# Two accumulator banks for projections and one for head turns, loads in four pieces, and GpSimd in the output rounding of a fused cross-attention kernel

## The reference: what is computed

```
ln_out = LN(x);  q, k, v, qx = fp8_linear(ln_out, each with its own input scale)   # rounded to e4m3
q, k, qx, kx = LN over each head of 128;  kx, vx from ctx @ w_kv_x (fp32)
core = softmax(q k^T / sqrt(128)) v;   xout = softmax(qx kx^T / sqrt(128)) vx      # 8 groups, 2 heads each
cat  = concat(core, xout);  catq = e4m3(bf16(clip(cat / smooth, -448, 448)))
x += tanh(g0) * (catq @ wproj^T) * scales
x += tanh(g1) * bitlinear(silu(gate) * up)
```

## Time and profile before

| | before |
|---|---|
| median of the runs | 1891.02 us |
| profiled execution, its own time | 1892.87 us |
| its span from first to last instruction | 1891.1 us |
| first and last score matmul start | 109.3 us, 1535.7 us |
| TensorE busy | 1640.8 us, 87% |
| VectorE busy | 1567.0 us, 83% |
| ScalarE busy | 1353.8 us, 72% |
| GpSimd busy | 1092.9 us, 58% |
| mean granted TensorE clock | 0.967 |

### The profile page before, as it was taken

One profiled execution on the slowest core, in us unless ns is written; L12 is line 12 of the kernel. 1 busy time (PEld: TensorE's weight loads), 2 busy tenths in 40 slices (PEclk: granted clock), 3 DMA queues, 4 the chain that ended last, 5 costly groups with the idle time before them and its releaser, 6 DMA issues.

```text
span 1891.1 us, 35124 instructions
## 1 busy us (share of the span) xinstructions
PE 1640.8 (87%) x11147; PEld 1012.6 (54%) x11164; DVE 1567.0 (83%) x3445; ACT 1353.8 (72%) x3351; POOL 1092.9 (58%) x1427
## 2 busy tenths in 40 slices
PE   1478888788989998889999888999999879999995
PEld 0355555555656665556666555666666524444442
DVE  7668888998888889978888998999988866777774
ACT  6468888777878987887898778999888852222222
POOL 3677887776777767776776567777676630000000
PEclk9879999999999999999999999999999999999997
DMA  2367888778999998889999997999999985422200
GB/s 97 106 151 152 188 186 188 170 175 179 217 217 203 208 216 187 184 184 211 208 225 193 209 199 177 223 234 230 220 212 187 194 176 207 111 79 73 73 18 17
DMA packets 667677, 325.48 MB, mean 172 GB/s; under 512 B 551904, under 2 KB 595040, under 8 KB 666720
## 3 DMA queue, kind: packets, MB, share of 16 engines
q1 hardware_dynamic: 667488, 323.17, 75.9%
HBM read 140.61 MB, written 48.23 MB: 100 GB/s over the span
## 4 chain that ended last, share of the span: by engine, by line
PE 34%; DVE 32%; POOL 13%; issue 8%; ACT 8%; DMA 3%; SPq 0%; POOLq 0%; ACTq 0%; DVEq 0%
DVE nmx L963 6%; DVE pp L973 6%; PE psum L736 6%; PE psum L711 6%; PE psum L682 5%; PE psum L694 5%; PE psum L649 4%; PE psum L656 3%; PE psum L753 3%; DMA pt<-pp 2%; POOL qk L1555 2%; POOL ars L1533 2%; DVE cc L985 2%; PE psum L669 2%; DVE xh L946 2%
## 5 line engine op out<-in xcount | busy, mean ns | idle before, releaser
L682 PE MATMUL psum<-qk 128*128 128x512 f16 x1536 | 426.5, 388 | 17.1 <-DVE pp L973 12.5
L649 PE MATMUL psum<-wbt,xqt 128*128 128x256 f16 (+1 forms) x4096 | 412.0, 251 | 23.8 <-POOL wbt L1502 13.4
L694 PE MATMUL psum<-pt,vv 128*128 128x512 f16 x1536 | 405.5, 388 | 31.0 <-ACT cy L1327 21.7
L1308 ACT ACTIVATE psum<-psum,nmx 128x512 f32<-128x512 f32 x512 | 343.1, 670 | 104.6 <-DVE nmx L963 102.8
L649 PEld LDWEIGHTS psum<-wbt,xqt 128*128 128x128 f16 x4096 | 334.1, 100 | 136.0 <-issue 21.8
L963 DVE TENSOR_REDUCE nmx<-psum 128x1 f32<-128x512 f32 x512 | 345.6, 675 | 58.7 <-PE psum L682 57.7
L973 DVE SCALAR_TENSOR_TENSOR pp<-psum,prs,pp 128x512 f16<-128x512 f32 x512 | 379.0, 740 | 7.1 <-ACT pp L1319 6.9
L1319 ACT ACTIVATE pp<-psum,prs 128x512 f16<-128x512 f32 x512 | 355.2, 694 | 14.8 <-DMA pt<-pp 14.4
L694 PEld LDWEIGHTS psum<-pt,vv 128*128 128x128 f16 x1536 | 151.1, 100 | 226.8 <-issue 57.0
L1555 POOL TENSOR_TENSOR qk<-y,qk 128x512 f16<-128x512 f32 x192 | 233.8, 1218 | 16.0
L656 PE MATMUL psum<-wbt,ctxh 128*128 128x256 f16 x1536 | 193.3, 277 | 8.7 <-POOL ctxh L1481 8.7
(11 more groups left out here) (175 smaller groups left out, 2696.1 us busy)
## 6 DMA issues: line engine op xcount, KB each, us to landing
wbt<-ws SPq DMA_DIRECT2D x192, 256.0 KB, 3.7
ws<-wbt SPq DMA_DIRECT2D x64, 256.0 KB, 4.0
catd<-cy SPq DMA_DIRECT2D x64, 256.0 KB, 3.4
raw<-in_wgu SPq DMA_DIRECT2D x64, 256.0 KB, 3.6
raw<-in_w SPq DMA_DIRECT2D x32, 384.0 KB, 3.8
wbt<-catd SPq DMA_DIRECT2D x6, 2048.0 KB, 9.9
pt<-pp SPq DMA_TRANSPOSE x512, 3.7
raw<-in_wp SPq DMA_DIRECT2D x32, 256.0 KB, 3.6
```

Source lines behind the costliest of these rows:

```text
L649: ins = e.matmul(bank[:, o0:o0 + c1 - c0], xv[:, v, kt * 512 + tt * 128:kt * 512 + (tt + 1) * 128], wb[i][:, h, kt, c0:c1], start=kt == 0 ...
L682: ins = e.matmul(SB(n), qk[i][:, jq, u, ss], qk[i][:, jk, w, :], start=k == 0, stop=k == 2)
L694: ins = e.matmul(OB, v[:, t, u, att, :], src[:, w, t, :], start=t == 0 and k == 0, stop=t == 3 and k == 2)
L1308: e.activation(SB(n), SB(n), ACT.Exp, bias=nmx[:, k], accum_out=psm[:, k]).then_inc(s["exp"], 1)
```

## The change

1. Banks: after slot -4 banks 5 and 6 hold A and B tiles alone, in turn, and bank 7 holds everything else (T, X, W, C, S, F). Before slot -4 the first list is 5, 6, 0, 1, 2, 3.
2. The loads of x and of the context are four DMAs of 256 KB each, in slots 1 to 4 and 62 to 65; who reads them waits for all four. The statistics of x move from slots 4, 6, 8, 10 to 6, 8, 9, 10.
3. The turns X move from slots 20, 36, 52, 60 to 20, 26, 36, 52; the context's factor `cxf` from slot 86 to 85.
4. ScalarE writes all four quarters of `ctxh` high in slot 102 (before: two in 102, two in 103). GpSimd makes two quarters of the low part in slot 102, VectorE the other two in slot 103.
5. `group_factors` moves from n modulo 16 = 7 to 4, and S and F readers (SCALE_AT, FLAG_AT) by one or two slots.
6. All output steps lie one slot later: clip at n modulo 8 = 2, field 3, step 4, add 5, sub 6 and 0, store 3. From pair 18 (group 9) on GpSimd makes the step, so 46 of the 64; new semaphores o_f and o_s link field, step and add.

```diff
-FACTORS_AT = 7
+FACTORS_AT = 4
...
-OUT_AT = {"clip": 17, "field": 18, "step": 19, "add": 20, "sub": (21, 23), "store": 26}
+OUT_AT = {"clip": 18, "field": 19, "step": 20, "add": 21, "sub": (22, 24), "store": 27}
+POOL_STEP = 9 * 2
 JOBS_FROM, TERN_FROM = 92, 309
-SCALE_AT = {"sum": 303, "whole": 308, "fac": 310}
-FLAG_AT = {"sum": 306, "whole": 324, "fac": 326}
+SCALE_AT = {"sum": 303, "whole": 307, "fac": 308}
+FLAG_AT = {"sum": 306, "whole": 324, "fac": 325}
 X_AT = {
-    "load": (1,),
-    "stats": (4, 6, 8, 10),
+    "load": (1, 2, 3, 4),
+    "stats": (6, 8, 9, 10),
     "rstd": (10,),
     "norm": (13, 14, 15, 16),
-    "turn": (20, 36, 52, 60),
-    "ctx": (62,),
+    "turn": (20, 26, 36, 52),
+    "ctx": (62, 63, 64, 65),
     "quant": tuple(range(62, 102)),
     "bound": (70, 72, 74, 76),
     "cxp": (82,),
     "cxs": (83,),
     "cxw": (84,),
-    "cxf": (86,),
+    "cxf": (85,),
     "mid": (90, 92, 94, 96),
-    "parts": (102, 102, 103, 103),
+    "parts": (102, 102, 102, 102),
...
-    turn = [5, 6, 7, 0, 1, 2, 3]
+    long, short = [5, 6, 0, 1, 2, 3], [7]
     for n, use in order:
         if n >= RAMP:
-            turn = [k for k in turn if k >= 5]
+            long = [k for k in long if k >= 5]
+        turn = long if use[0] in "AB" else short
         k = turn.pop(0)
         turn.append(k)
         bank[use] = k
...
-            def load_x(b):
+            def load_x(b, t):
                 q.wait_ge("cx_lo", 4 * b)
-                e.dma_start(xt[:], x[b * S:(b + 1) * S, :].rearrange("(t p) d -> p t d", p=128)).then_inc(s["x_ld"], 16)
-
-            def load_ctx(b):
+                e.dma_start(xt[:, t, :], x[b * S + t * 128:b * S + (t + 1) * 128, :]).then_inc(s["x_ld"], 16)
+
+            def load_ctx(b, kt):
                 q.wait_ge("x_tr", 4 * b + 4)
-                e.dma_start(xt[:], ctx[b]).then_inc(s["ctx_ld"], 16)
+                e.dma_start(xt[:, kt, :], ctx[b][:, kt, :]).then_inc(s["ctx_ld"], 16)
...
+            def ctx_lo(b, kt):
+                q.wait_ge("cx_hi", 4 * b + kt + 1)
+                e.tensor_tensor(ctxh[:, 1, kt, :], xt[:, kt, :], ctxh[:, 0, kt, :], ALU.subtract).then_inc(s["cx_lo"], 1)
...
-            def out_step(pair, step):
-
-                y, tmp = cy[pair % 3][:], cc[:]
+            def out_field(pair):
+
                 q.wait_ge("o_c", pair + 1)
-                q.wait_ge("o_w", 3 * pair + step)
-                if step == 0:
-                    q.wait_ge("o_q", 2 * pair)
-                    ins = e.tensor_scalar(tmp.bitcast(U16), y.bitcast(U16), 0x7F80, None, ALU.bitwise_and)
-                elif step == 1:
-                    ins = e.tensor_scalar(tmp, tmp, 24.0, 0.375, ALU.mult, ALU.max)
-                else:
-                    ins = e.tensor_tensor(y, y, tmp, ALU.add)
-                ins.then_inc(s["o_w"], 1)
+                q.wait_ge("o_q", 2 * pair)
+                e.tensor_scalar(cc[:].bitcast(U16), cy[pair % 3][:].bitcast(U16), 0x7F80, None, ALU.bitwise_and).then_inc(s["o_f"], 1)
+
+            def out_step(pair):
+                q.wait_ge("o_f", pair + 1)
+                e.tensor_scalar(cc[:], cc[:], 24.0, 0.375, ALU.mult, ALU.max).then_inc(s["o_s"], 1)
+
+            def out_add(pair):
+                q.wait_ge("o_s", pair + 1)
+                e.tensor_tensor(cy[pair % 3][:], cy[pair % 3][:], cc[:], ALU.add).then_inc(s["o_w"], 1)
...
-                for k, step in enumerate(("field", "step", "add")):
-                    for pair in pairs_at(n, OUT_AT[step]):
-                        out_step(pair, k)
+                for pair in pairs_at(n, OUT_AT["field"]):
+                    out_field(pair)
+                for pair in pairs_at(n, OUT_AT["step"]):
+                    if pair < POOL_STEP:
+                        out_step(pair)
+                for pair in pairs_at(n, OUT_AT["add"]):
+                    out_add(pair)
...
+                for b, kt in x_steps(n - 1, "parts"):
+                    if kt >= 2:
+                        ctx_lo(b, kt)
...
+            def out_step(pair):
+
+                q.wait_ge("o_f", pair + 1)
+                e.tensor_scalar(cc[:], cc[:], 24.0, 0.375, ALU.mult, ALU.max).then_inc(s["o_s"], 1)
...
-                q.wait_ge("o_w", hc // 2 * 3 + 3)
+                q.wait_ge("o_w", hc // 2 + 1)
...
+                for pair in pairs_at(n, OUT_AT["step"]):
+                    if pair >= POOL_STEP:
+                        out_step(pair)
...
-                    ctx_lo(b, kt)
+                    if kt < 2:
+                        ctx_lo(b, kt)
```

More of the change, by code:

```diff
@@ L267 @@
     "ga gb vh vx_lo a_st b_st a_rs b_rs a_n b_n b_na hd_tr y32 hd_hi hd_lo "
-    "scores mx exp rc sc hi lo tr0 tr1 tr2 tr3 pv o_y o_c o_w o_q "
+    "scores mx exp rc sc hi lo tr0 tr1 tr2 tr3 pv o_y o_c o_f o_s o_w o_q "
     "l_sum l_r l_ar l_sc l_t1 l_t2 l_hi l_lo l_ab l_fr l_fa flag "
@@ L496, in sp_program @@
                 e.dma_start(dst, src).then_inc(s["const"], 16)
-            load_x(0)
+            for t in range(4):
+                load_x(0, t)
             for t in range(4):
                 load_raw(0, t)
-            load_ctx(0)
+            for kt in range(4):
+                load_ctx(0, kt)
             load_raw(0, 4)
@@ L521, in sp_program @@
                         store_w(it, k)
-                for b, _ in x_steps(n, "load"):
-                    load_x(b)
-                for b, _ in x_steps(n, "ctx"):
-                    load_ctx(b)
+                for b, t in x_steps(n, "load"):
+                    load_x(b, t)
+                for b, kt in x_steps(n, "ctx"):
+                    load_ctx(b, kt)
                 if n in JOB_AT and JOB_AT[n] < 0:
@@ L827, in ctx_part @@
             def ctx_part(b, kt):
-                q.wait_ge("ctx_ld", 16 * (b + 1))
+                q.wait_ge("ctx_ld", 64 * (b + 1))
                 q.wait_ge("cxp", b)
@@ L873, in x_stats @@
                 if t == 0:
-                    q.wait_ge("x_ld", 16 * (b + 1))
+                    q.wait_ge("x_ld", 64 * (b + 1))
                 q.wait_ge("x_rs", b)
```

## The result

The changed kernel takes 2000.92 us (median of four runs, 1999.08 to 2002.27) and the kernel before 1891.66 us beside it: a ratio of 1.058 (95% interval 1.056 to 1.060), 109 us slower. The forecast was 1846 us and "faster".

What follows compares the result with a forecast made beforehand. TensorE was taken as the floor, VectorE as the bound in rounds rounding a new x, no engine full elsewhere. Sum -33 + 9 - 8 + 1 - 8 - 6 - 2 + 1 + 1 = -45: 1891.0 to 1846 us; 8-in-10 range 1815 to 1876.

Steps and rivals of the forecast that it cites:

- signs that were to show the forecast wrong: Early rounds as long with other releasers; VectorE idle over 0.5 us before the add; VectorE-bound rounds not shorter.
- the VectorE-bound rounds: Rounds that round a new x to e4m3, VectorE busy 89.0 of 90.7 and 92.9 of 93.4 us; should shorten.
- The step's duration: Output step moved to GpSimd: 1.06 us each, as the clip; gain 6 us, between 0 and 12.
- The round trip: Rival, 7%: VectorE's add waits in order behind GpSimd's step, late by one more head, 1.8 us a step; 1901 us.
- the add comes just as the step ends: Normal slot: GpSimd's step ends 2.66 us after the statistics, just when VectorE finishes normalising and reaches the add.
- The banks: Banks 5 and 6 for A and B alone end TensorE's normalising waits: -33 us (14 early, 16 from 514 to 1191 us, 3 quiet).
- the neighbour X: Bank 7, X between two T: the T of slot 28 waits for ScalarE, +3 us in three batches, +9 (0 to +36).
- the waits move: Rival, 23%: TensorE runs into the scores' or PV's wait instead; banks give 12 instead of 33; -24, 1867 us.
- Loads: Loads of x and context in four pieces, no megabyte ahead of the probabilities' DMAs: -8 us, and +1 at the start.
- context parts: GpSimd's share of ctxh ends with its first pair, so TensorE's B-tile wait goes three times: -8 us (0 to 12).
- factors, small moves: Group factors three slots up, ahead of rstd no longer, plus cxf, scale and flag moves: -2 us for all.
- The loop's end: Last pair's add before L1035, its step 1.06 instead of 0.41 us and two handovers: +1 us.

## Why the prediction was wrong

Read backwards, the changed kernel's way from 1891.7 to 2000.9 us is: banks and the rest with X at 26, down to 1864.6 (25 to 27 us); the later output slots, +23; the step on GpSimd, +113. Three of the signs that were to show the forecast wrong stand in the profile: VectorE idle in front of the add by 2.75 us, the step at 3.63 us, the VectorE-bound rounds not shorter.

- **The step's duration** failed first. The sentence "GpSimd needs 1.06 us for an instruction of this shape, the clip" took the price from the same engine, shape and type but another pair of operations. Measured: 3.63 us, not 1.06. I gave 0 to 12 us of gain as its bounds; only gain, although no row showed mult/max on GpSimd. And 6 us were not there at 1.04 us either: the relief of VectorE, 35.9 us of its instructions, was half given back as its other instructions became longer, and the time did not fall (1869.23 for 1864.59). The rstd power in the earlier trace rows (1.04 us for 4 values) was a warning that there the operation counts and not the size.
- **The round trip** was the rival with the right mechanism: VectorE stands in order at the add. I gave it 7% and 1901 us, and let one more head on GpSimd decide it, not the step's own length. It predicted 1.8 us a step (83 us); 2.75 us (126.5 us) were found. At the assumed price it is small: 15.3 us of waiting in 33 adds, against my "the add comes just as the step ends"; the move then costs 12 us at the late slots and is worth nothing (+5, not told apart from 0) at the old ones, where I had -6. That this kernel's 1899.75 lies near the rival's 1901 is chance, since about 23 us of it come from the slots.
- **The output one slot later** isn't in the sum at all. I followed the step and not the clip, though the rule of the argument was to price everything that is moved. Alone it costs 40 us in the kernel before, 23 in the changed one; the clip's place makes 17 of these. How the other 6 come about wasn't followed.
- **The two errors cost more together than apart.** With the slow step the late slots cost 2000.92 - 1925.60 = 75 us, with VectorE's step 23. Apart, step and slots make 61 + 23 = 84 us, together 136. In the late slots step and clip both stand behind an rstd that waits for VectorE; that this makes the whole 52 us is argued and not tried.
- **The banks** were right in kind and too large in size. -33 + 9 = -24 was the term with the neighbour X; -23.5 us was measured for the ring and X at 26 together (1888.10 to 1864.59), and 21 to 24 for the ring alone. That the sum of the two came out is luck. The +9 was there, 8.7 us in the rounds with slot 26, but the sum had nothing for the rounds that were rid of slot 60 and gave it back. And not three X were waited for but 11 of the 12, 16.5 us in all. The -33 fell short in one place. The first batch (slots 0 to 127), with -14, became 16.3 us shorter, in the kernel with banks alone against before and in the one with X at 60 against the one without the banks alike. Slots 128 to 367, with -16, became shorter by 1.7 and 6.4 us, the rest, with -3, changed by +1.2 and -4.4. (These are single profiled executions; that of the kernel with banks alone was 7.5 us above its median.) The rival "the waits move" saw this in kind: its 12 was too little. Why so little arrives from slot 128 on stays open.
- **Loads, context parts, factors, small moves**: -8 + 1 - 8 - 2 = -17 forecast, about -1 measured (interval -5 to +2). The named waits went (6.5 to 1.2 us at the loads, 8.7 to 0 at `ctxh`); what they were worth did not arrive. The gain in the early rounds is the banks' alone: their 154.8 us became 147.5 with the banks alone and 154.6 with all but the banks. Why nothing arrives isn't known; whether VectorE's share of the context parts takes the gain wasn't tried. (The loads of x became 16 DMAs for 4, so three more a batch for x and three for the context, not six each; SP's share is nothing either way.)
- **The loop's end**, +1 for the last pair, was about 3: the wait for the last x (L1044 in the profile after) is 7.5 us for 4.2 before. This is the step's price again: with the step at 1.04 us it is 4.9, with the step on VectorE 4.2.

Without the step and the slots my sum would have been -40, and -25 to -27 came; these two made 136 us of the other sign, of which my range held none. In that kernel (1864.59 us) the quiet round of slot 384 takes 39.2 us, as was foretold of the banks.

## What to carry to other kernels

Price an instruction by a row with the same engine, shape, type and operations; where no such row exists, one run of the bare instruction settles it, and until then the upper bound must not be its look-alike. When work moves a slot, follow every instruction that moves, not only the one the change is about, and ask what each comes to stand behind on its in-order engine: an instruction behind one that waits for the very engine that needs the result makes a loop between two engines. Do not count a named wait that goes as gained time: here about half of the 43.9 us arrived that the banks' waits outside the VectorE-bound rounds were, and nothing that can be told of the loads' and the context parts'. And an instruction that leaves one engine can lengthen that engine's others: half of what VectorE was relieved of came back.

## What was not expected of the hardware

GpSimd's tensor_scalar has three prices for one shape: 128 x 1024 values take 1.04 us with min/max or mult/mult, 3.62 us with mult/max, max/mult or max/max, and 2.77 us with mult or max alone, which is slower than the fast pairs of two. The pairs cost the same in bf16 and fp32 (mult/max, mult/mult and min/max were tried), and mult/max the same alone and beside work (3.624 to 3.656 us in all 46 steps). VectorE shows nothing of the kind: with GpSimd idle, 0.43 us in bf16 and 0.69 in fp32 for every form tried. At 512 values mult/max takes 1.92 us on GpSimd, about half, so by these two sizes the slow form costs per value and not at its start.
